# A transformer decoder layer in fp32: projections written out, the first matrices turned between products, the output projection of self attention joined with the queries

## What is computed

```python
x = x + _L0_attn_ref(_layernorm(x), q_heads, k_heads, v_heads, output_proj)       # causal, x @ W.T
x = x + _L0_xattn_ref(_layernorm(x), ctx_1024, W_q, W_k, W_v, W_o, b_o)           # x @ W
x = x + _L0_ffn_ref(_layernorm(x), gate_W, gate_b, W1, b1, g1, be1, W2, b2, g2, be2)   # best 2 of 4 experts
```

## Time and profile before

| | us |
|---|---|
| median of 3 runs | 4449.33 (4442.33 to 4449.73) |
| the profiled execution | 4446.99 |
| its span, from the first to the last instruction | 4445.3 |
| TensorE busy in it | 4010.5 |
| first projection, first load to last product | 3.7 to 331.9 |
| output projection, first load to the next stage's first load | 1071.7 to 1185.7 |
| queries, the same | 1185.7 to 1334.3 |
| keys and values, first load to last product | 1334.3 to 1738.3 |

### The profile page before, as it was taken

The page is one execution under the profiler, slowest core; times in us unless marked ns, Lnnn a source line. Parts: engine busy times, 40 slices in busy tenths (PEclk is TensorE's granted clock), DMA queues, the critical chain, the costliest instruction groups (busy, mean ns, idle before and its releaser), DMA issues. The chain is left out here.

```text
span 4445.3 us, 60825 instructions
## 1 busy us (share of the span) xinstructions
PE 4010.5 (90%) x21522; PEld 2473.0 (56%) x21522; DVE 2727.0 (61%) x4963; ACT 2095.5 (47%) x3870; POOL 2589.9 (58%) x963
## 2 busy tenths in 40 slices
PE   6997999997788998999999999999999967349997
PEld 5874555554676886444444444444444445238885
DVE  4435777772453334877777777777777525336765
ACT  2112555553122111566666666666666634226665
POOL 0003455454000001699999999999999935618887
PEclk8996999998898998899999999999999978669998
DMA  4546454422555556122222222222222036434444
GB/s 145 179 156 145 107 113 90 107 48 87 206 193 180 174 171 170 34 58 58 58 58 58 58 58 58 58 58 58 58 58 58 6 144 137 76 105 81 80 83 62
DMA packets 275062, 432.66 MB, mean 97 GB/s; under 512 B 31689, under 2 KB 132041, under 8 KB 268618
## 3 DMA queue, kind: packets, MB, share of 16 engines
q1 hardware_dynamic: 251050, 390.23, 33.6%
q0 software_dynamic: 19776, 36.85, 4.9%
q10 hardware_dynamic: 3968, 2.10, 0.2%
HBM read 258.57 MB, written 170.52 MB: 97 GB/s over the span
## 5 line engine op out<-in xcount | busy, mean ns | idle before, releaser
L881 DVE TENSOR_REDUCE cross_neg_max<-cross_scores 128x1 f32<-128x512 f32 x2048 | 1264.8, 676 | 396.0 <-PE cross_scores L708 395.9
L665 POOL TENSOR_TENSOR cross_partial<-cross_partial,cross_probs 128x2048 f32<-128x2048 f32 x320 | 1465.6, 4580 | 66.7 <-ACT cross_probs L832 29.6
L832 ACT ACTIVATE cross_probs<-cross_shifted 128x512 f32<-128x512 f32 x2048 | 1074.1, 606 | 742.3 <-PE cross_shifted L720 707.6
L708 PE MATMUL cross_scores<-cross_k_stack,cross_q_stack 96*128 96x512 f32 x2048 | 875.9, 437 | 39.7 <-DVE cross_neg_max L881 27.4
L720 PE MATMUL cross_shifted<-cross_q_stack,cross_k_stack 98*128 98x512 f32 x2048 | 850.7, 420 | 13.9 <-ACT cross_probs L832 6.1
L720 PEld LDWEIGHTS cross_shifted<-cross_q_stack,cross_k_stack 98*128 98x128 f32 x2048 | 387.1, 190 | 385.5 <-issue 233.6
L708 PEld LDWEIGHTS cross_scores<-cross_k_stack,cross_q_stack 96*128 96x128 f32 x2048 | 395.2, 193 | 286.6 <-DVE cross_neg_max L881 224.1
L832 ACT ACTIVATE self_probs<-self_shifted 128x512 f32<-128x512 f32 (+3 forms) x768 | 358.8, 492 | 348.4 <-PE self_shifted L723 266.9
L881 DVE TENSOR_REDUCE self_neg_max<-self_scores 128x1 f32<-128x512 f32 (+3 forms) x768 | 388.0, 547 | 187.1 <-PE self_scores L708 96.2
L736 PE MATMUL cross_out<-cross_probs,cross_v 128*32 128x512 f32 x4096 | 492.7, 598 | 0.0
L708 PE MATMUL self_scores<-self_k_stack,self_q_stack 96*128 96x512 f32 (+3 forms) x768 | 308.3, 423 | 21.0 <-DMA self_k_stack<-k_hi 9.8
(11 more groups left out here) (268 smaller groups left out, 6113.9 us busy)
## 6 DMA issues: line engine op xcount, KB each, us to landing
cross_k_stack<-k_hi SPq DMA_DIRECT2D x30, 1024.0 KB, 20.0
kv_x_in<-in_ctx SPq DMA_DIRECT2D x16, 1024.0 KB, 5.5
k_hi<-kv_out_hi SPq DMA_DIRECT2D x64, 256.0 KB, 2.6
k_lo<-kv_out_lo SPq DMA_DIRECT2D x64, 256.0 KB, 3.2
v<-kv_out_n SPq DMA_DIRECT2D x64, 256.0 KB, 2.3
cross_v<-v SPq DMA_DIRECT2D x32, 512.0 KB, 25.1
self_q_stack<-q_hi SPq DMA_DIRECT2D x30, 512.0 KB, 6.9
self_k_stack<-k_hi SPq DMA_DIRECT2D x30, 512.0 KB, 15.2
```

Source lines behind the costliest of these rows:

```text
L665: nc.gpsimd.tensor_tensor(total, total, own, ALU.add).then_inc(pool_added.sem, 1)
L708: mm = nc.tensor.matmul(scores[at][:, 0:width], q_st[0:96, w, h, q0:q0 + P], k_st[0:96, w, h, half * WIDE:half * WIDE + width], start=True ...
L832: nc.scalar.activation(probs[:, e % NE % PB, h, f:], shifted[n % SHIFTED][:, f:], ACT.Exp).then_inc(exped.sem, 1)
L881: nc.vector.tensor_reduce(neg_max[:, q % 2, column(a), half:half + 1], scores[n % (SLOTS * ROUNDS) % AHEAD][:, 0:width], AX.X, ALU.max, ne ...
```

## The change

`load_weights` is gone. In `project` everything is straight code. The matrices of "qkv1" are loaded whole (three buffers, chunk 0 of the tokens second in the queue), and turned a quarter at a time through the two PSUM tiles of the tokens, with splits of a quarter: matrix 0 before chunk 0, matrices 1 and 2 between the products of chunk 0 (`turn_at`), where product 4 and product 8 wait for the whole of theirs. The moments and the normalising of chunk 1 are queued on VectorE behind the splits of chunk 0 and ahead of those of matrix 1.

`bridge` takes the place of "out1" and "q2": it adds the projected attention into the residual in SBUF, stores that as `x1` and normalises it without a reload, with the output projection two chunks ahead of the queries. It has one buffer each for `a_hi`, `a_lo`, `xt_hi` and `xt_lo`, three for the residual. The normalising is on ScalarE. It also splits the two matrices of "kv2", which stay in SBUF (`kv_hi`, `kv_lo`), so that "kv2" loads no matrix.

The diff, cut to its core:

```diff
-def load_weights(nc, name, weights, hi, lo, ident, first_loads):
...
+def project(nc, name, src, chunks, norm, weights, outs, ident, neg_half, split=None):
...
+    LAST = BATCH * chunks
+    turning = 0 if split else len(weights)
...
-        TURN = {t * NOUT // TPC: t for t in range(TPC)}
-
-        def passes(eng, chunk):
-
-            with eng.Fori(0, BATCH - 1) as it:
-                for u in range(chunks):
-                    chunk(it, u, True)
-            for u in range(chunks):
-                chunk(BATCH - 1, u, False)
...
+        def turn_at(u, n):
+
+            if u == 0 and turning:
+                return ("matrix", n // KT + 1, n % KT) if n < KT * (turning - 1) else ("tokens", 1, n - KT * (turning - 1))
+            if n % (NOUT // TPC) == 0 and u + 1 < LAST:
+                return "tokens", u + 1, n // (NOUT // TPC)
+            return None
...
+            def load_matrix(m):
+                sp.dma_start(raw[:, m], weights[m][0].rearrange("(k p) n -> p k n", p=P)).then_inc(raw_loaded[m], 16)
+
+            if turning:
+                load_matrix(0)
+            load(0)
+            for m in range(1, turning):
+                load_matrix(m)
+            load(1)
+            for u in range(LAST):
...
+            if norm:
+                variance(0)
+            for k in range(KT if turning else 0):
+                matrix_low(0, k)
+            if norm:
+                normalise(0)
+            for t in range(TPC):
+                tokens_low(0, t)
+            if norm:
+                variance(1)
...
+            def turn_matrix(m, k):
+                if k == 0:
+                    pe.wait_ge(raw_loaded[m], 16)
+                after(pe, lo_ready, matrix_at(m) + k - 1)
+                for q in range(KT):
+                    mm = nc.tensor.transpose(turned[k % 2][:, q, :], raw[:, m, q, k * P:(k + 1) * P], ident[:, :])
+                mm.then_inc(turned_ready, 1)
...
+                    if u == 0 and n and g == 0 and turning:
+                        pe.wait_ge(lo_ready, matrix_at(w) + KT)
+                    after(pe, out_lo_ready, u * NOUT + n - 3)
...
-def project_out(nc, name, attn_t, weight, bias, residual, out, ident):
+def bridge(nc, name, attn_t, out_w, residual, x1, q_w, q_out, q_scale, next_w, next_hi, next_lo, ident, neg_half):
...
+        a_hi = sb("a_hi", [P, KT, CH], F32R)
+        a_lo = sb("a_lo", [P, KT, CH], F32R)
+        x_in = sb("x_in", [P, 3, TPC, D])
...
+            def load(c):
+                if c >= 3:
+                    sp.wait_ge(x_stored[c % 3], 16 * (c // 3))
+                    sp.wait_ge(normed, TPC * (c - 2))
+                sp.dma_start(x_in[:, c % 3], tiles_of(residual)[c]).then_inc(loaded[c % 3], 16)
+
+            sp.dma_start(raw[:, 0], weight_rows(out_w)).then_inc(raw_loaded[0], 16)
+            load_attention(0)
+            load(0)
+            sp.dma_start(raw[:, 1], weight_rows(q_w)).then_inc(raw_loaded[1], 16)
+            load_attention(1)
+            load(1)
+            load_attention(2)
+            load(2)
+            sp.wait_ge(ow_lo_ready, KT)
+            sp.dma_start(raw[:, 0], weight_rows(next_w[0])).then_inc(raw_loaded[0], 16)
+            sp.wait_ge(qw_lo_ready, 1)
+            sp.dma_start(raw[:, 1], weight_rows(next_w[1])).then_inc(raw_loaded[1], 16)
+            for c in range(CHUNKS):
+                sp.wait_ge(added, TPC * (c + 1))
+                sp.dma_start(tiles_of(x1)[c], x_in[:, c % 3]).then_inc(x_stored[c % 3], 16)
+                if c + 3 < CHUNKS:
+                    load_attention(c + 3)
+                    load(c + 3)
+                for n in range(HG):
+                    sp.wait_ge(out_lo_ready, HG * c + n + 1)
+                    tok = slice(c % 2 * CH, (c % 2 + 1) * CH)
+                    for part, src in ((0, out_hi), (1, out_lo)):
+                        sp.dma_start(q_out[part][c // 2 * HG + n, :, tok], src[:, n].bitcast(F32)).then_inc(q_stored[n], 16)
...
+            def attention_high(c):
+                act.wait_ge(a_loaded[c % 2], 16 * (c // 2 + 1))
+                after(act, acc_ready, TPC * c)
+                nc.scalar.activation(a_hi[:, :, :], a_in[:, c % 2], ACT.Copy).then_inc(a_hi_ready, 1)
+
+            def normalise(c):
+                act.wait_ge(scaled, c + 1)
+                after(act, turned_ready, TPC * (c - 1))
+                for t in range(TPC):
+                    nc.scalar.activation(x_n[:, c % 2, t], x_in[:, c % 3, t], ACT.Identity, scale=rstd[:, t:t + 1],
+                                         bias=shift[:, t:t + 1]).then_inc(normed, 1)
+
+            def next_high(m):
+                act.wait_ge(raw_loaded[m], 32)
+                nc.scalar.activation(next_hi[:, m], raw[:, m], ACT.Copy).then_inc(next_hi_ready, 1)
+
+            for k in range(KT):
+                act.wait_ge(w_turned, k + 1)
+                nc.scalar.activation(ow_hi[:, k], q_acc[k][:, :], ACT.Copy).then_inc(ow_hi_ready, 1)
+            attention_high(0)
+            act.wait_ge(raw_loaded[1], 16)
+            nc.scalar.activation(qw_hi[:, :, :], raw[:, 1], ACT.Copy).then_inc(qw_hi_ready, 1)
+            attention_high(1)
+            normalise(0)
+            attention_high(2)
+            for c in range(CHUNKS):
+                after(act, q_ready, HG * c)
+                for t in range(TPC):
+                    act.wait_ge(turned_ready, TPC * c + t + 1)
+                    nc.scalar.activation(xt_hi[:, :, t * P:(t + 1) * P], turned[t % 2][:, :, :], ACT.Copy).then_inc(hi_ready, 1)
+                if c + 1 < CHUNKS:
+                    normalise(c + 1)
+                if c + 3 < CHUNKS:
+                    attention_high(c + 3)
+                if c in (2, 4):
+                    next_high(c // 2 - 1)
+                for n in range(HG):
+                    act.wait_ge(q_ready, HG * c + n + 1)
+                    after(act, q_stored[n], 32 * c)
+                    nc.scalar.activation(out_hi[:, n], q_acc[n][:, :], ACT.Copy, scale=q_scale).then_inc(out_hi_ready, 1)
...
+            for k in range(KT):
+                dve.wait_ge(ow_hi_ready, k + 1)
+                nc.vector.tensor_tensor(ow_lo[:, k], q_acc[k][:, :], ow_hi[:, k].bitcast(F32), ALU.subtract).then_inc(ow_lo_ready, 1)
+            attention_low(0)
+            dve.wait_ge(qw_hi_ready, 1)
+            nc.vector.tensor_tensor(qw_lo[:, :, :], raw[:, 1], qw_hi[:, :, :].bitcast(F32), ALU.subtract).then_inc(qw_lo_ready, 1)
+            for t in range(TPC):
+                add_projection(0, t)
+            attention_low(1)
+            variance(0)
+            scales(0)
+            for t in range(TPC):
+                add_projection(1, t)
+            attention_low(2)
+            for c in range(CHUNKS):
+                for t in range(TPC):
+                    dve.wait_ge(hi_ready, TPC * c + t + 1)
+                    nc.vector.tensor_tensor(xt_lo[:, :, t * P:(t + 1) * P], turned[t % 2][:, :, :],
+                                            xt_hi[:, :, t * P:(t + 1) * P].bitcast(F32), ALU.subtract).then_inc(lo_ready, 1)
+                    if t == 0 and c + 1 < CHUNKS:
+                        variance(c + 1)
+                    if t and c + 2 < CHUNKS:
+                        add_projection(c + 2, t - 1)
+                if c + 1 < CHUNKS:
+                    scales(c + 1)
+                if c + 2 < CHUNKS:
+                    add_projection(c + 2, TPC - 1)
+                if c + 3 < CHUNKS:
+                    attention_low(c + 3)
+                if c in (2, 4):
+                    next_low(c // 2 - 1)
+                for n in range(HG):
+                    dve.wait_ge(out_hi_ready, HG * c + n + 1)
+                    after(dve, q_stored[n], 32 * c)
+                    nc.vector.scalar_tensor_tensor(out_lo[:, n], q_acc[n][:, :], q_scale, out_hi[:, n].bitcast(F32),
+                                                   ALU.mult, ALU.subtract).then_inc(out_lo_ready, 1)
...
+            def project_tile(c, t):
+                if t == 0:
+                    pe.wait_ge(a_lo_ready, c + 1)
+                after(pe, added, TPC * c + t - 1)
+                i = 0
+                for part, w in ((a_hi, ow_hi), (a_hi, ow_lo), (a_lo, ow_hi)):
+                    for k in range(KT):
+                        mm = nc.tensor.matmul(acc[t % 2][:, :], part[:, k, t * P:(t + 1) * P], w[:, k, :], start=i == 0, stop=i == 11)
+                        i += 1
+                mm.then_inc(acc_ready, 1)
...
+            pe.wait_ge(raw_loaded[0], 16)
+            for k in range(KT):
+                for m in range(KT):
+                    mm = nc.tensor.transpose(q_acc[k][:, m * P:(m + 1) * P], raw[:, 0, m, k * P:(k + 1) * P], ident[:, :])
+                mm.then_inc(w_turned, 1)
+            pe.wait_ge(ow_lo_ready, KT)
+            for t in range(2 * TPC):
+                project_tile(t // TPC, t % TPC)
+            for c in range(CHUNKS):
+                for t in range(TPC):
+                    turn_tile(c, t)
```

(20 more changed lines are left out.)

510 lines of the change are left out of this document (234 added, 276 removed).

## The result

The changed kernel takes 4396.8 us (median of 4 runs, 4393.2 to 4400.5), the kernel before 4445.9 us (4 runs, 4442.3 to 4449.7) beside it: a ratio of 0.989, 95% interval 0.987 to 0.991, 49.1 us less. The forecast was 4395 us, within 4382 to 4417. The profiled execution after took 4396.94 us, its span 4395.2.

A forecast was written before the change was run, and what follows sets the result against it. TensorE was taken as the bound, busy 4010.5 of 4445.3 us, with idle time at stage starts. 19.9 + 25.5 + 7.9 = 53.3 us off 4446.99 gives 4393.7, on the median 4396; 4395 was taken, range 4382 to 4417.

The forecast's parts named there:

- First projection: Stage "qkv1": loop of products starts at 25.7 instead of 49.75 us; net gain 19.9 us, ends 12 and 22.
- What is given back: First stage: eight turns now between products and a possible wait of product 4 cost 4.1 us of the 24.0 gained.
- Joined stage: `bridge`, output projection with queries: 237.1 us instead of 262.6, gain 25.5 us, ends 35 and -10.
- the period: Time of one steady chunk in `bridge`: 23.9 us, taken for chunks 1 to 5, with no wait for the split.
- Keys and values: Stage "kv2": no matrices to load, first product 12.3 us after the first load; gain 7.9 us, ends 6 and 9.
- Self attention: Attention stage after the first projection, outside the change: keeps its length, 0 us.
- Straight code: Written-out code instead of `Fori` loops: no gain and no visible price, bounds -0.9 and +1 us.
- Rival 1: `bridge`: single `a_hi` stalls steady chunks as in `finish`; 4431 at full price, 4413 at half; chance 0.14.
- Rival 2: First stage: chunk 0 of the tokens lands at 17 to 20 us, gain only 12 to 15, 4402; chance 0.10.
- rival 3: New straight code: TensorE waits at each code block, slower above 1.8 us each, 4470 at 2.5 us; chance 0.05.
- Rival 4: `bridge` does better: restarts and chunk 6 nearly free, chunk 0 dense; gain 63, 4385; chance 0.10.
- Rival 5: First stage: early turns queue behind VectorE's chunk 1 work, TensorE starts no earlier; 24 us less, 4419; chance 0.04.

The follow-up runs named there:

- two-buffer kernel: The changed kernel with two buffers each for `a_hi` and `a_lo`, and chunks 1 and 2 of the attention split earlier: 4381.2 us, ratio 0.986.
- late moments: The changed kernel with the moments of chunk 7 moved behind the four low splits of chunk 6 in `bridge`: 4384.5 us, ratio 0.988.
- landing order: The changed kernel with the first chunk of tokens loaded behind all three matrices instead of behind the first: 4394.4 us.

## Why the prediction was right

- **First projection** (19.9 predicted, 20.0 measured; first loop turn 25.7 predicted, 25.56 measured). The chain held step by step: tokens in at 12.0 (11.8), moments done at 15.0 (15.1), normalised and split by 25.5. The wait of 4.46 us at 15.75 was inside that chain, which had the parts of the matrix behind the moments. What is given back was put at 4.1 us; the gain fell from 24.2 at the first turn to 20.0 at the first score, so 4.2. That sum is right by terms that are not. A turn costs 0.45 us between products, so eight are 3.6; the forecast had 0.38 as its lower value because it took the values' products at 2.80 us, and they took 2.75. Product 4 did not wait for its matrix. In its place the first product ran at 1.2 GHz for longer: its fours start 1.86 and 1.70 us apart and the next turn 1.60 us after the third, where the old kernel has 1.86, 1.69 and 0.93, so 0.7 us more.
- **Joined stage** (25.5 predicted, 24.6 measured). From its first load: first product 13.7 us (14.2), end of the first wait 31.6 (32.2), of the second 48.8 (50.2), end of chunk 0 73.5 (74.8), period 23.95 (23.9), end of chunk 5 193.3 (194.3), of chunk 6 214.9 (215.3), next stage's load 238.0 (237.1). The use of `finish` as the price list was the decision that carried this: its 4.39 and 3.51 us became 4.39 and 3.52. The two-buffer kernel shows that this is the cause. Two terms of the clock were off and partly cancel: the first four matmuls behind the two waits took 1.52 and 1.60 us, not the 2.08 of `finish`, and the slow clock behind the waits of chunk 7 was left out (23.1 us from its start to the next stage's first load, forecast 21.8; with the late moments, at the full clock, 21.6). The least certain term, counted five times, was the period; the kernel with added VectorE work shows how near it was to being wrong: 1.15 us of room.
- **Keys and values** (7.9 predicted, 8.2 measured): right in sum, by two misses that cancel, and one of them is luck. The first product is 11.8 us after the load (12.3), and it starts at the full clock (four matmuls in 1.17 us), which the forecast did not count. Against that, the pace of the values cost 16 x 0.14 = 2.2 us, which it could not see. In the three traces with the same placement whose products began at 1.2 GHz (two buffers, added VectorE work, late moments) the stage lasts 410.0 to 410.6 us, a gain of 5.4 to 6.0: at or under the lower end of 6.
- **Self attention** (0 predicted, +2.1 measured). The forecast kept its length without a reason. The traces with the new first projection have 731.4 to 738.2 us there against 730.1 to 732.0, with more waiting for `self_v`; so this term was probably too small by some us, and in this trace by little.
- **Straight code** (0 within -0.9 to +1): measured alone, 0.2 us, within the interval of zero.
- **Rivals.** Rival 1 has the right mechanism and is confined to the start of the stage, where the forecast already had it. Rival 2 fell with the landing order, rival 3 with straight code alone. Rival 4 (4385) is what two buffers or the later moments give, not this change. Rival 5 is refuted by the first turn at 25.56.
- The stages sum to 52.8 us; the span is 50.1 shorter. The 2.7 us between are self attention (2.1) and the rest (0.6, of a stretch that moves by up to 14.8 us from trace to trace).

## What to carry to other kernels

When two stages are joined, look for a stage of the same kernel that already has the same buffers and waits: its rows price the new start and tell whether a wait survives where more work covers it. Read steady chunks for the one instruction that stands nearest to a wait, not for the busy share: 13 to 15 of 24 us busy left 1.15 us of room here. When a stage starts earlier, look at what the next one waits for: part of the gain may stay there. And try the stationary and the moving operand of dense matmuls at the same offset modulo 128 bytes; unused tiles of 32 and 64 bytes took 12 us off three stages here.

## What the runs showed of the hardware

- The pace of four matmuls of 128x512 depends on where both operands lie in SBUF: 0.907 us at equal places modulo 128 bytes, 0.915 or 0.933 otherwise, as steady as 24.14, 24.00 and 23.69 us a chunk in three kernels. At 96 and 32 it was 0.915 in most chunks and 0.933 in the last.
- Waits of 1.23 and 1.41 us with turns between them left the next four matmuls at 1.89 us in one execution (granted clock 1.2 GHz) and at 1.20 us in another (2.4 GHz). Where they came behind waits of 2.96 and 1.41 us, it was 2.08.
- The first four matmuls of keys and values took 1.17 to 1.21 us in three traces and 2.05 or 2.06 us (1.2 GHz) in six, behind much the same in all nine: a wait of 10.6 to 11.2 us for a load, then turns with waits of 0.56 and 1.41 to 1.53 us.
- Loads of 1 MB issued together land in the order of issue, 2.7 us apart (12.01 and 17.38 us for the second and the fourth of them).
- Loops' back-jumps and their straight form took the same time within 0.1%.
